# Turning adj inside the attention layer: VectorE squares and 128-byte stores instead of TensorE transposes in layer 3

## What is computed

```python
# layer 1 of 4: attention, 4 heads of 64, adj is bias and mask
scores = einsum('hnd,hmd->hnm', q, k) * 64**-0.5 + graph_bias * adj
scores = where(adj == 0, -1e9, scores)
out = einsum('hnm,hmd->hnd', softmax(scores), v) @ Wout + bout
# layer 2: graph attention
Wh = x @ W;  e = leaky_relu((Wh @ a[:256])[:, None] + (Wh @ a[256:])[None, :], 0.2)
out = softmax(where((adj > 0) | eye, e, -9e15), axis=1) @ Wh
# layer 3 and layer 4: normalised aggregation, d = adj.sum(1) ** -0.5
out3 = (d[:, None] * adj * d[None, :]) @ x @ W2.T + b2
out4 = relu((d[:, None] * adj * d[None, :]) @ x @ W3)
```

## Time and profile before

| | us |
|---|---|
| median of 3 runs | 3217.26 |
| lowest, highest | 3213.86, 3217.59 |
| the profiled execution | 3217.47 |
| its span, first to last instruction | 3215.7 |
| PE busy in the span | 3125.0 |
| DVE, ACT busy | 2020.4, 2034.8 |

### The profile page before, as it was taken

How to read it: one execution, slowest core, us unless ns; L and a number is a source line. 1 busy time by engine, 2 the same in 40 slices (tenths; PEclk the granted TensorE clock), 3 DMA queues, 4 the chain that set the end, 5 groups by cost and what they waited for, 6 DMA issues and landing times.

```text
span 3215.7 us, 49326 instructions
## 1 busy us (share of the span) xinstructions
PE 3125.0 (97%) x17636; PEld 2272.7 (71%) x17636; DVE 2020.4 (63%) x3510; ACT 2034.8 (63%) x3097; POOL 363.9 (11%) x198
## 2 busy tenths in 40 slices
PE   8899999999999999999998999999999999999998
PEld 5677777777777777777765555555688888778886
DVE  6666666666676666766648877776344444655554
ACT  3677777777777777777766776776555555633332
POOL 2000000000000000000004555544000000000000
PEclk9999999999999999999999999999999999999999
DMA  6322333223333223332272333331588788855541
GB/s 184 92 66 86 99 103 102 80 73 97 102 102 99 68 83 102 102 103 76 74 263 84 135 132 137 138 124 56 197 303 284 270 287 300 290 204 214 201 184 71
DMA packets 152702, 463.86 MB, mean 144 GB/s; under 512 B 13168, under 2 KB 49008, under 8 KB 136048
## 3 DMA queue, kind: packets, MB, share of 16 engines
q1 hardware_dynamic: 146160, 439.40, 40.5%
q0 software_dynamic: 6272, 20.98, 2.1%
HBM read 372.25 MB, written 88.08 MB: 143 GB/s over the span
## 4 chain that ended last, share of the span: by engine, by line
PE 84%; DVE 6%; DMA 3%; issue 3%; ACT 2%; SPq 0%; DVEq 0%; POOL 0%; POOLq 0%; ACTq 0%
PE at_score L459 14%; PE at_o L484 13%; PE gl_four L1278 12%; PE at_turn L471 11%; PE gl_quad L1357 4%; PE gl_quad L1359 4%; PE gl_quad L1358 4%; PE gl_quad L1261 3%; PE gl_four L1319 3%; PE gl_four L1321 3%; PE gl_four L1320 3%; PE gl_quad L1303 3%; DVE at_probs L703 2%; DMA at_bias<-in_adj 2%; PE gl_four L1333 2%
## 5 line engine op out<-in xcount | busy, mean ns | idle before, releaser
L703 DVE CUSTOM_DVE_ANT_0 at_probs<-at_score,at_bias 128x1024 f32<-128x1024 f32 x508 | 621.7, 1224 | 487.0 <-PE at_score L459 481.7
L598 ACT ACTIVATE at_pT<-at_turn 128x1024 f32<-128x1024 f32 x512 | 522.1, 1020 | 333.7 <-PE at_turn L471 333.0
L459 PE MATMUL at_score<-at_kT,at_q 128*128 128x512 f32 x2032 | 609.4, 421 | 26.8 <-DVE at_maxima L703 19.9
L589 ACT ACTIVATE at_probs<-at_probs,at_minus_max 128x1024 f32<-128x1024 f32 x512 | 585.1, 1143 | 9.6 <-DVE at_minus_max L708 8.7
L484 PE MATMUL at_o<-at_pT,at_values 128*64 128x256 f32 x4096 | 498.3, 385 | 0.0
L471 PE MATMUL at_turn<-all_ident,at_probs 128*128 128x128 f32 x4096 | 489.1, 272 | 0.0
L471 PEld LDWEIGHTS at_turn<-all_ident,at_probs 128*128 128x128 f32 x4096 | 462.3, 140 | 35.8 <-issue 1.9
L1278 PE MATMUL gl_four<-gl_early,gl_first_wh 128*128 128x512 f32 x1024 | 462.6, 595 | 1.4 <-ACT gl_early L1442 1.4
L459 PEld LDWEIGHTS at_score<-at_kT,at_q 128*128 128x128 f32 x2032 | 349.8, 188 | 144.0 <-DVE at_maxima L703 78.1
L484 PEld LDWEIGHTS at_o<-at_pT,at_values 128*64 128x64 f32 x4096 | 271.2, 136 | 202.6 <-issue 91.0
L1676 DVE TENSOR_TENSOR gl_lo<-gl_quad,gl_hi 128x512 fp32r<-128x512 f32 x256 | 175.2, 691 | 249.9 <-ACT gl_kept_kept L1468 248.7
(11 more groups left out here) (130 smaller groups left out, 3883.6 us busy)
## 6 DMA issues: line engine op xcount, KB each, us to landing
at_bias<-in_adj SPq DMA_DIRECT2D x128, 512.0 KB, 5.2
at_values<-v_heads SPq DMA_DIRECT2D x256, 256.0 KB, 3.2
gl_first_weights<-in_adj SPq DMA_DIRECT2D x32, 2048.0 KB, 7.9
gl_units<-in_adj SPq DMA_DIRECT2D x32, 2048.0 KB, 9.5
adjT<-gl_kept_kept SPq DMA_DIRECT2D x64, 1024.0 KB, 10.1
gl_units<-adjT SPq DMA_DIRECT2D x64, 1024.0 KB, 4.8
gl_early<-x SPq DMA_DIRECT2D x24, 512.0 KB, 7.2
x<-gl_early POOLq DMA_DIRECT2D x16, 512.0 KB, 4.3
```

The costliest lines, as they stand in the source:

```text
L459: last = pe.matmul(place[:, at], q[:, q_place(h), part, t * P:(t + 1) * P], kT[:, h, col:col + BANK], start=part == 0, stop=part == 1)
L589: act.activation(part, part, ACT.Exp, bias=minus_max[:, k, t:t + 1], scale=1.0, accum_out=sums[:, k, t, pp:pp + 1]).then_inc(prob_ready, 1)
L598: act.activation(pT[:, j % PT_SLOTS, :], turn_bank[j % 2][:], ACT.Copy).then_inc(pT_ready, 1)
L703: dve.tensor_tensor_reduce(out=probs[:, k, t, at], in0=place[:], in1=bias[:, t, at], scale=SCALE, scalar=LOWEST, op0=ALU.add, op1=ALU.max, ...
```

## The change

1. **adj is turned in layer 1.** A block is 128 rows by 512 columns of adj; there are 16 to a chunk, 256 in all. SP loads it (128 pieces of 2 KB) into a place called `squares`; DVE turns it with one `transpose`, which turns each 32x32 square where it stands; SP stores it in four transfers (one for each 32 partitions) whose pieces are 128 bytes long, which put each square at its place in `adjT`. `adjT` now has 32 rows of 2 MB. There are 1,024 such stores, of 512 pieces each. A block is turned in every odd beat (in the last chunk in 16 of its first 24), after the beat's other work.
2. **Seven places for probabilities** instead of eight make the room for `squares`, and `AHEAD` becomes 12; `BIAS_LOAD` and `BIAS_PARTS` move two beats later.
3. **The loop over chunks is written out** in all engines.
4. **Layer 3 runs as layer 4 does:** 16 runs (`RUNS`) of 16 pairs with one code. No transposes, no high and plain copies of turned tiles, no stores of them. `split3` has six places instead of four. A set of 1 MB comes in four transfers of 32 partitions with pieces of 2 KB, where layer 4 had one transfer of 128 partitions with pieces of 8 KB.
5. **The scaled rows** are no longer made by DVE and then copied by ACT: ACT scales while it copies (`split_hi`) and DVE scales while it subtracts (`split_lo`, one instruction in place of two).
6. **A new border:** W and a are loaded first (into `dst_row`), DVE sums 12 row pieces instead of 8, from beat 24 on; maxima, the shift and the first exponentials come earlier among the Wh steps; the first three splits of layer 3 are made in the last pairs of layer 2.

```diff
-    AHEAD = 14
+    AHEAD = 12
+    PLACES = 7
+    BLOCK_BEATS = tuple(range(1, CHUNK_BEATS, 2))
+    LAST_BLOCK_BEATS = (1, 2, 4, 5, 7, 8, 10, 11, 13, 14, 16, 17, 19, 20, 22, 23)
...
+            def store_block(b):
+                row_tile, n = block_at(b)
+                sync.wait_ge(block_turned, b + 1)
+                to = adjT.rearrange("j (s k r) -> j s k r", k=BLOCK_TILES * SQUARES, r=BLOCK)
+                for g in range(SQUARES):
+                    at = row_tile % BLOCK_TILES * P + g * SQUARE
+                    sync.dma_start(to[:, row_tile // BLOCK_TILES * BLOCK_SETS + n, :, at:at + SQUARE],
+                                   squares[g * SQUARE:(g + 1) * SQUARE, 1, b % 2, :]
+                                   .rearrange("j (k i) -> j k i", i=SQUARE))\
+                        .then_inc(block_stored[b % 2], 16)
...
+            def turn_block(b):
+                dve.wait_ge(block_loaded[b % 2], 16 * (b // 2 + 1))
+                wait(dve, block_stored[b % 2], 16 * SQUARES * (b // 2))
+                dve.transpose(squares[:, 1, b % 2, :], squares[:, 0, b % 2, :]).then_inc(block_turned, 1)
...
-                wait(dve, turned, BEATS * (u - 2) + CT * (pp + 1))
+                wait(dve, turned, CT * (PIECES * u + pp - PLACES + 1))
...
+                for q in range(SQUARES):
+                    sync.dma_start(tiles[q * SQUARE:(q + 1) * SQUARE, n, :].rearrange("j (k r) -> j k r", k=KEPT),
+                                   kept[q, :, SETS * (r % CHUNKS) + n, :, :]).then_inc(tiles_loaded[n], 16)
...
-    adjT = nc.dram_tensor("adjT", [P, N * N // P], F32, kind="Internal").ap()
+    adjT = nc.dram_tensor("adjT", [32, N * N // 32], F32, kind="Internal").ap()
```

More of the change, by code:

```diff
@@ L270, in chunks @@
         def chunks(eng, body):
[L272 to L276 removed]
+            for c in range(CHUNKS):
+                body(c, c == CHUNKS - 1)
         def piece_at(i):
@@ L354, in sync_program @@
                 load_values(0, q)
+            sync.wait_ge(run_turned, RUNS)
+            for b in range(2):
+                load_block(b)
             def body(c, last):
@@ L391, in finish @@
                 pool.dma_start(x1_tiles[:, bass.ds(c * CT, CT), :], acc[:]).then_inc(x1_stored, 16)
-            finish(0)
-            with pool.Fori(1, CHUNKS) as c:
+            for c in range(CHUNKS):
                 finish(c)
@@ L806, in graph_layers @@
     CHUNKS = N // CN
-    STEPS = NT
     PAIRS = NT // 2
@@ L1760, in vector_program @@
             read_max(17)
-            for e in range(11, LEAD - 3):
+            for e in range(13, LEAD - 3):
                 logits(e)
@@ L1823, in vector_program @@
-            keep_out(dve, dve.tensor_copy, 1, 2, CHUNKS - 1)
+            for r in range(RUNS):
+                layer, c = layer_and_chunk(r - 1)
+                quick = r in (0, CHUNKS)
+                for pair in range(PAIRS):
+                    if r or pair >= len(EARLY_SPLITS):
+                        read_lo3(r, pair)
+                    if pair == 1:
+                        keep_out(dve, dve.tensor_copy, 1, CHUNKS + r - 1)
+                    if r == 0 and pair == 4:
+                        add_out(CHUNKS - 1)
+                    if r == CHUNKS and pair == 4:
+                        add_rows(layer, c)
+                    if not quick and pair in (6, 7):
+                        add_relu(layer, c, (2 * pair - 12, 2 * pair - 11))
+                    if not quick and pair == 8:
+                        add_old(layer, c)
+                    if not quick and pair == 9:
+                        ln.statistics(dve, y, CHUNKS * layer + c)
+                    if pair == (6 if quick else 11):
+                        ln.normalise(dve, y, CHUNKS + r - 1)
+                    for k in rows_at(r, pair):
+                        split_lo(k)
```

571 lines of the change are left out of this document (233 added, 338 removed).

## The result

Before: 3216.2 us median (3213.9 to 3217.6). After: **3176.3 us** (3172.7 to 3183.6). The ratio is 0.9881, with a 95% interval from 0.9869 to 0.9893: 40 us or 1.2% faster. The prediction was 3077, its range 3048 to 3170: the sign is right, and the time lies 6 us beyond the range, with 100 of the 141 us of gain missing. The profiled execution's span is 3170.9 us.

What follows compares the result with a forecast made beforehand. PE's row of instructions was taken to set the time everywhere. Layers 3 and 4 -151, joint +3, layer 1 +25 (+23 + 8 - 6) and border -18 gave -141 on 3217.5: 3077 us, range 3048 to 3170.

Steps and rivals of the forecast that it cites:

- Layers 3 and 4, -151: Layers 3 and 4: both become 16 runs of layer 4's kind at 46.6 us each, a gain of 151 us.
- The joint, +3 (0 to 10): Layer 3's last run and the joints: scaled rows and layer norm crowd DVE, ACT's lead shrinks; 3 us given back.
- The turn, 0.62 us and +23: Layer 1: each turn takes DVE 0.62 us, and crowded DVE makes PE idle longer in each chunk; +23 us.
- The queues' price: Layer 1 DMA queues: 20 ns per 128-byte store piece, 86 of 100 us busy a chunk, so the queues hold.
- inside the slack, mostly: Layer 1 bias stretch: two beats carry 6.9 us of transfers, a backlog of some 5 us mostly absorbed; +8 us (0 to 60).
- rival B: Layer 1: stores cost 23 to 29 ns or block loads come late, holding up score reads; +50, 3130 us, chance 0.10.
- Seven places and AHEAD 12, taken at nothing, and the loops, -6: Layer 1: fewer places leave the same wait, costing nothing; written-out loops save PE's issue waits, -6 us.
- a unit's slack (24 us), so they hide: Layer 1 values loads: they have a unit's slack, 24 us, so their delay behind other transfers hides.
- The border, -18: Border from layer 1 to 2: W and a come first and the shift waits less; -18 us (-5 to -28).
- Rival A: Layer 1: 128-byte stores become the new bound, at 32 ns a piece, and the kernel is slower; 3250 us, chance 0.14.
- Rival C: Layers 3 and 4: set loads to 32 partitions give 170 GB/s and bind the runs; +78, 3155 us, chance 0.07.
- Rival D: Layer 1: the turn costs DVE twice the expected price; +24, 3101 us, chance 0.07.

Runs made afterwards that it cites:

- rows_early: Changed kernel with the row tiles of layer 3's last run fetched ahead of the set load, and seven xs places instead of four; 3151.2 us.
- best_c: best_b with the bias parts spread so that beats 16, 20 and 24 hold one part instead of two; 3135.1 us.
- no_turn: Changed kernel with DVE touching one column of a block instead of turning it, and the wait for stores moved to SP; 3165.9 us.
- bf_no_turn: bias_first with DVE touching one column of a block instead of turning it, and the wait for stores on SP; 3168.3 us.
- bf_no_stores: bias_first without the 1,024 stores of turned blocks, block loads and turns kept; 3127.8 us.
- nb_bias_first: no_blocks with SP's bias load put first in each beat; 3111.8 us.
- no_blocks: Changed kernel without layer 1's block loads, turns and stores; layers 3 and 4 read adj itself; 3130.8 us.
- values_ahead: Changed kernel with adj piece 2 and x of the border loaded only behind the last values load, row sums about one beat later; 3177.2 us.
- bias_first: Changed kernel with SP's bias load put first in each beat, ahead of stores, block load and values load; 3174.8 us.
- best_b: Changed kernel with bias loads first in a beat, row tiles of layer 3's last run fetched early, and block loads ahead of stores; 3139.0 us.
- best_d: best_c with a chunk's eight bias loads spread over beats 12 to 22 instead of 12 to 19; 3138.6 us.

## Why the prediction was wrong, step by step

- **Layers 3 and 4, -151: right in the steady state.** 210 matmuls in 47.0 us as worked out, no waits of PE in a run other than at the joint. **The joint, +3 (0 to 10), was the failed step**: it counted DVE's work and ACT's lead there and not SP's order. The row tiles stand behind set loads that wait for DVE, and DVE waits for the row tiles. The loss was 35 us over the sum's 746; rows_early takes 25 of it back, best_c 30 (layers 3 and 4 in 751.0 us). Some 10 us of the loss aren't waits but PE's lower clock between them.
- **The turn, 0.62 us and +23.** It took 0.71. Its worth by no_turn and bf_no_turn is 0.4 to 0.7 us a chunk, 6 to 11 us, and with the block loads it is 16 at most (bf_no_stores): less than the term. The prediction took all of DVE's work over PE's pace as PE's loss; what absorbs the rest stays open.
- **The queues' price: right. What it means: the failed step.** 20 ns a piece was forecast, 22 measured; a share near 0.85 forecast, 0.84 to 0.88 measured. But a share over a chunk decides nothing, as the share of busy engines didn't. In the bias stretch it is 0.9 to 1.05. The prediction had 6.9 us of queue in 5.7 us there and called it "inside the slack, mostly", +8. The slack was two beats for the bias and three for a block, and none was left: 2.3 us a chunk for the pieces, and 44 in the whole with the last chunk. This is rival B's mechanism, late transfers that hold up DVE, at 22 ns, just under the 23 of its first condition; but in the changed kernel it was the bias that came late (55.5 us) and hardly the blocks (2.8).
- **Seven places and AHEAD 12, taken at nothing, and the loops, -6.** Together nothing (98.76). PE's 6.1 us of "issue" waits went as forecast, but in nb_bias_first its waits for score reads are 26.9 us against 13.8. The bias moved by two beats with the places, to a shorter pair: 1.2 us a chunk while nothing else is late.
- **Values: "a unit's slack (24 us), so they hide": a failed step.** Wrong in the last chunk, which with the border makes the largest gap, 43 us. SP reached the last of them at 1727.79, after 13.21 and 5.84 us of issuing stores, with the border's loads ahead in the queues. Of the 22.4 us, 10.4 stand in no_blocks too and are the border's own order; a lower clock follows. From the last x load to the last aggregate it takes 187.2 us, 166.1 without blocks (nb_bias_first) and 150.7 before: 15 us are the new border's, which stood in no term, and 21 the blocks'.
- **The border, -18.** -10 measured. values_ahead shows that it is tied to the last chunk by the order of the loads: of the 15.5 us that the chunk won there, the border lost 13.4.
- **Rival A** (31 ns and more) didn't come: 22. **Rival C** neither: 47.0 us a run with 32-partition loads, though the queues are full. A share of 1.00 goes with 216 GB/s in a steady run, and 1.01 with 230 in rows_early's first window. The 249 GB/s of the earlier trace rows was misread as the rate of 64-partition loads: the two loads of Wout (L345) are 512 pieces, at most half of the 1,090 packets of 20:25 (in 12:16, with much the same piece sizes, the queues moved 366 GB/s). The estimate of 215 worked out from the Trainium skill, "SBUF — State Buffer" (Door 1: The DMA port swizzle), is near the 216, but the 230 lies above it, so no run shows a ceiling there. C's own sum had 2.5 us for 1 MB of other traffic, 400 GB/s, which no row has. **Rival D** (turn at twice the price) didn't come.
- **The range** held each failure singly (B at 3130, C at 3155) but not two of them at once: the joint, at 35 us, was in no case at more than 10, and layer 1 lay 54 over its term. That the time came within 6 us of the range's end is no merit of the sum: three terms failed, all one way.

Not settled: how the border would go with the last chunk's blocks elsewhere at an even spacing, and whether the 128-byte pieces cost by their size or by their places in HBM. No run had these apart.

## What to carry to other kernels

A transfer's slack runs from the moment the issuing queue reaches it, not from when its place comes free: for each moved load, list what stands ahead of it on that queue and what those wait for, and look for a loop back through the engine that it feeds. Take the DMA share in the busiest few microseconds, not over the loop; where it is near 1 there, as here at 0.9 to 1.05, slack won't hide what is added, and moving loads about moved the wait in every try (bias_first, best_b, best_d). When one wait is removed and nothing is gained, take the parts away again from there: on top of the late bias the stores looked worth 0.6 us a chunk, and without it 2.3. And price the last pass of a loop by itself, where other work already stands in the queues.

## What the hardware showed

- Stores in 128-byte pieces cost the queues 22 ns a piece, three times what the same bytes cost in 2 KB pieces (44.0% against 14.0% of 16 x 200 us), and 9 ns of it lie on other packets, reads of 2 KB beside them. The Trainium skill, "DMA: Bandwidth & Descriptors" (Specifications), puts line rate at 512 bytes and above: the trace agrees, with three times the cost at 128.
- Issuing on SP isn't free or constant: a store of 512 pieces takes 0.51 us, one of 32 pieces 0.42, and four of them 13.2 us where the queues are full.
- A 32x32-square turn of 128x512 float32 takes 0.71 us, about what a copy of that size takes (0.685 in the earlier trace rows).
- After PE's waits of 6.84 and 15.51 us in the last chunk the next aggregate took 3.68 us for 1.95, each time; the granted clock was 0.50 in 1730:1740.
